# A half-width sort with the rest counted apart, and gathers in threes that wait for TensorE's experts instead of for their own landing

## The reference, cut to what matters

```python
h = (x_flat @ W_gat).reshape(M, 4, 4)
src = concatenate([edge_index[0], loops]); dst = concatenate([edge_index[1], loops])
e = leaky_relu(a_src[src] + a_dst[dst], 0.2)
ee = exp(e - segment_max(e, dst)[dst])
denom = segment_sum(ee, dst)
agg = segment_sum(h[src] * (ee / denom[dst])[:, :, None], dst) + b_gat
scores = layernorm(agg).mean over heads      # then top 2 of 4 experts, softmax
out = sum over experts of gate * (gelu(x @ W1[e] + b1[e]) @ W2[e] + b2[e])
```

## Time and profile before

| | us |
|---|---|
| median of 3 runs | 3851.6 |
| profiled execution | 3831.2 |
| its span, first to last instruction | 3829.6 |
| busy: VectorE | 2878.4 (75%) |
| busy: TensorE, matmuls | 2611.3 (68%) |
| busy: ScalarE | 1816.2 (47%) |
| busy: GpSimd | 1133.4 (30%) |
| mean granted TensorE clock | 0.842 of full speed |

### The profile page before, as it was taken

One profiled execution on the slowest core, in us unless ns is written; L12 is line 12 of the kernel. 1 busy time (PEld: TensorE's weight loads), 2 busy tenths in 40 slices (PEclk: granted clock), 3 DMA queues, 4 the chain that ended last, 5 costly groups with the idle time before them and its releaser, 6 DMA issues.

```text
span 3829.6 us, 50716 instructions
## 1 busy us (share of the span) xinstructions
PE 2611.3 (68%) x16023; PEld 1941.3 (51%) x16024; DVE 2878.4 (75%) x7979; ACT 1816.2 (47%) x3236; POOL 1133.4 (30%) x1200
## 2 busy tenths in 40 slices
PE   2888888888888720015667677676776767676689
PEld 1666666666666510013445455455554545455566
DVE  7999898988898652347777778777777787687774
ACT  1666666666666401112444445344444544444444
POOL 0000000000000014555545555455545555455400
PEclk7999999999999965556878788787878878788889
DMA  2111111111110123222222223223222222322200
GB/s 86 36 48 39 45 39 45 36 36 45 37 47 28 65 23 85 47 60 55 57 73 64 72 61 75 61 59 75 58 72 65 61 71 64 71 61 57 73 12 9
DMA packets 241379, 208.18 MB, mean 54 GB/s; under 512 B 86460, under 2 KB 174168, under 8 KB 240600
## 3 DMA queue, kind: packets, MB, share of 16 engines
q1 hardware_dynamic: 186984, 188.72, 16.9%
q0 software_dynamic: 37152, 14.34, 3.8%
q10 hardware_dynamic: 16976, 1.89, 0.6%
HBM read 158.15 MB, written 46.67 MB: 53 GB/s over the span
## 4 chain that ended last, share of the span: by engine, by line
POOL 23%; DMA 19%; issue 16%; PE 3%; DVE 2%; ACT 0%; POOLq 0%; DVEq 0%
POOL lay_got L1514 23%; DMA lay_got<-node_table,lay_idx 19%; PE lay_b_y L1563 1%; PE lay_b_z L1554 1%; DVE keep_x L1904 0%; DVE lay_xn L1939 0%; DVE lay_stats L1928 0%; POOLq L1512 0%; PE lay_b_b L1593 0%; ACT lay_att L1742 0%; PE lay_b_g L1627 0%; ACT L1686 0%; ACT lay_hid L1686 0%; PE lay_b_g L1643 0%; PE lay_b_g L1635 0%
## 5 line engine op out<-in xcount | busy, mean ns | idle before, releaser
L1514 POOL DMA_INDIRECT lay_got<-node_table,lay_idx x1152 | 1114.3, 967 | 1061.8 <-DMA lay_got<-node_table,lay_idx 827.4
L1563 PEld LDWEIGHTS lay_b_y<-lay_w,lay_hid 128*128 128x128 f32 x4096 | 547.0, 209 | 242.8 <-issue 198.3
L1686 ACT ACTIVATE lay_hid<-lay_b_z,lay_b 128x512 f32<-128x512 f32 x512 | 335.6, 682 | 597.4 <-PE lay_b_z L1554 580.7
L1563 PE MATMUL lay_b_y<-lay_w,lay_hid 128*128 128x128 f32 x4096 | 548.2, 291 | 77.7 <-DVE keep_x L1904 61.6
L1554 PE MATMUL lay_b_z<-lay_xin,lay_w 128*128 128x512 f32 x1024 | 591.6, 707 | 2.0 <-ACT lay_hid L1686 2.0
L191 DVE TENSOR_TENSOR sort_keys<-sort_keys 128x1024 f32<-128x1024 f32 (+1 forms) x272 | 399.0, 1467 | 11.3 <-DVE front_rms L109 0.5
L1540 PE MATMUL lay_b_att<-lay_parts,lay_oh 128*128 128x60 bf16 x1152 | 69.1, 215 | 494.5 <-DVE lay_parts L970 491.5
L192 DVE TENSOR_TENSOR sort_keys<-sort_keys 128x1024 f32<-128x1024 f32 (+1 forms) x272 | 397.4, 1461 | 0.0
L801 POOL MEMSET find_no_src<- 128x9 int32 x1 | 0.1, 108 | 1322.1 <-POOLq L46 1322.1
L1764 ACT ACTIVATE lay_unused<-lay_hub_wide,lay_halves 128x1152 bf16<-128x1152 uint16 x256 | 319.9, 1250 | 140.9 <-DMA lay_hub_wide<-sorted_dst 136.6
L961 DVE TENSOR_REDUCE lay_look<-lay_b_att 128x36 f32<-128x108 f32 x128 | 34.1, 267 | 446.3 <-DMA lay_got<-node_table,lay_idx 445.8
(11 more groups left out here) (344 smaller groups left out, 4832.2 us busy)
## 6 DMA issues: line engine op xcount, KB each, us to landing
lay_wide<-sorted_dst SPq DMA_DIRECT2D x128, 288.0 KB
lay_hub_wide<-sorted_dst SPq DMA_DIRECT2D x128, 288.0 KB
made<-front_y SPq DMA_DIRECT2D x128, 256.0 KB, 2.0
lay_y<-made SPq DMA_DIRECT2D x32, 1024.0 KB, 7.5
lay_got<-node_table,lay_idx POOLq DMA_INDIRECT x1152
front_adj<-in_adj SPq DMA_DIRECT2D x32, 256.0 KB, 3.1
keep_x<-in_x SPq DMA_DIRECT2D x32, 256.0 KB, 3.4
lay_adj<-in_adj SPq DMA_DIRECT2D x32, 256.0 KB
```

The costliest lines, as they stand in the source:

```text
L1514: pool.indirect_dma_start(out=got[:, b % RING, c, :], out_offset=None, in_=table, in_offset=bass.IndirectOffsetOnAxis(ap=idx[:, b % AHEAD, ...
L1563: mm = pe.matmul(b_y[n % 2][:, P * j:P * j + P], hid[n % 2][:, c, P * j:P * j + P], w2[:, e * HK + c, :], start=(c == 0), stop=(c == HK - 1))
L1686: act.activation(hid[n % 2][:, c, :], b_z[c][:, :], ACT.Gelu, bias=b1[:, e * HK + c:e * HK + c + 1]).then_inc(hid_ready, 1)
```

## The change

**The sort at half width.** `Network` now takes 2048 columns and 18 bits. The stages inside a row still sort all 4096 columns, as two halves of 2048. One stage of distance 2048 then leaves the 2048 lowest keys of each row in the left half; the right half is the rest. `set_aside` brings the 128 lowest keys of the rest to its front. Only the left half goes through the 7 levels across rows. Within a part between two turnings only the first and the last stage are taken by halves of 1024, the others whole. TensorE turns 2 quarters for each half instead of 4.

```diff
+            pos = self.run(pos, 0, 2 * cols, [1 << j for j in reversed(range(k))], first=True, directed=True)
+        pos = self.run(pos, 0, 2 * cols, [cols], first=True)
+        for kind, n in (("rest", 2 * cols), ("sign", cols // 2)):
...
+def set_aside(v, me, bufs, scratch, net, pos):
+    here, at = bufs[pos][:, net.cols:], 0
+    n = net.cols // 2
+    while n >= P:
+        low = bufs[1 - pos][:, net.cols:net.cols + P] if n == P else scratch[:, at:at + n]
+        me.mark(v.tensor_tensor(low, here[:, 0:n], here[:, n:2 * n], ALU.min))
+        me.mark(v.tensor_tensor(bufs[1 - pos][:, net.cols + n:net.cols + 2 * n], here[:, 0:n], here[:, n:2 * n], ALU.max))
+        me.wait()
+        here, at, n = low, at + n, n // 2
...
-                    for q in range(4):
+                    for q in range(net.quarters):
```

**The edge tables** store the far terms of each node too, and run a loop over the columns of the rest before the old loop:

```diff
+            act.wait_ge(exps_done, 3)
+            act.dma_start(rest_far[0:nodes, :].rearrange("(t n) f -> n t f", n=P), far[:, :, :]).then_inc(far_out, 16)
             act.wait_ge(table_out, 16)
             act.dma_start(hub_row[:, :], table[nodes - 1:nodes, :].broadcast_to([P, TAB])).then_inc(hub_in, 16)
+            n = rest_count_of(act)
+            with act.Fori(0, n) as g:
+                act.wait_ge(rest_step, 4 * g + 1)
+                act.dma_start(rest_key[:, :], rest_keys[:, bass.ds(g, 1)], allow_slow_non_contiguous=True)\
...
+            with pool.Fori(0, n) as g:
+                pool.wait_ge(rest_step, 4 * g + 2)
+                for out, array, at, got_it in ((rest_row, table, rest_src, rest_got[0]),
+                                               (rest_far_of, rest_far, rest_dst, rest_got[1]),
+                                               (rest_sum_of, rest_sums, rest_dst, rest_got[2])):
+                    pool.indirect_dma_start(
...
+                pool.wait_ge(rest_step, 4 * g + 4)
+                pool.indirect_dma_start(
+                    out=rest_sums, out_offset=bass.IndirectOffsetOnAxis(ap=rest_dst[:, 0:1].bitcast(U32), axis=0),
+                    in_=rest_msg[:, :], in_offset=None).then_inc(rest_out, 16)
+                pool.wait_ge(rest_out, 16 * g + 16)
```

**The layers** add `rest_sums` in the scores (a load of 8 blocks' rows by SyncE and one addition by VectorE), and count the hub edges set aside in rounds -1 and 0: VectorE makes two one-hots of 8 x 128 columns 16 times, TensorE multiplies them in 8 matmuls each into the bank `b_b`, and VectorE adds the result to `more_hub`. The gathers:

```diff
+                n = E1 * ((b - RING - 2) // 4 - QUAD - 2) + 2 * ((b - RING - 2) % 4)
                 for c in range(GC):
+                    if c % 3 == 0 and c > 0:
+                        after(pool, z_done, HK * min(n + 1 + c // 3, groups * E1) if n >= 0 else 0)
                     pool.indirect_dma_start(
                         out=got[:, b % RING, c, :], out_offset=None, in_=table,
                         in_offset=bass.IndirectOffsetOnAxis(ap=idx[:, b % AHEAD, c:c + 1].bitcast(U32), axis=0))\
                         .then_inc(gathered[b % RING], 16)
-
-                    if c % 3 == 2:
-                        pool.wait_ge(gathered[b % RING], (16 * GC) * (b // RING) + 16 * (c + 1))
```

More of the change, by code:

```diff
@@ L140, in __init__ @@
-        for k in levels:
-            t = len(self.holds)
-            self.holds.append(pos)
-            for h in range(2):
-                after = self.run(1 - pos, h * half, half, [1 << j for j in reversed(range(k - row_bits))],
-                                 directed=k < bits, turn=8 * t + 4 * h + 4)
-            after = self.run(after, 0, cols, [half], first=False)
-            pos = self.halves(after, half, [P << j for j in reversed(range(4))])
+            pos = self.run(pos, 0, 2 * cols, [1 << j for j in reversed(range(k))], first=True, directed=True)
@@ new lines, in __init__ @@
+        pos = self.run(pos, 0, 2 * cols, [cols], first=True)
+        self.rest = 1 - pos
+        for kind, n in (("rest", 2 * cols), ("sign", cols // 2)):
+            self.stages.append(Stage(self.total, pos, 0, n, 0, False, False, 0, False, kind))
+            self.total += n
+        pos = self.ends(1 - pos, [1 << j for j in reversed(range(row_bits))], turned=0)
+        for k in range(row_bits + 1, bits + 1):
+            self.holds.append(pos)
+            pos = self.ends(1 - pos, [1 << j for j in reversed(range(k - row_bits))]
+                            + [P << j for j in reversed(range(row_bits - 7))],
+                            turned=2 * len(self.holds) - 2, first=True, directed=k < bits)
@@ L149, in __init__, with run @@
             self.holds.append(pos)
-            pos = self.halves(1 - pos, half, [1 << j for j in reversed(range(7)) if k < bits or 1 << j >= LOOSE],
-                              turn=8 * t + 8)
+            pos = self.ends(1 - pos, [1 << j for j in reversed(range(7)) if k < bits or 1 << j >= LOOSE],
+                            turned=2 * len(self.holds) - 2)
         self.final = pos
         self.turned_from = [s.start for s in self.stages if s.half]
-    def run(self, pos, lo, n, distances, first=True, directed=False, turn=0, half=False):
+    def run(self, pos, lo, n, distances, first=False, directed=False, turn=0, half=False):
@@ L161, in run, with ends @@
         return pos
-    def halves(self, pos, half, distances, turn=0):
-        for h in range(2):
-            after = self.run(pos, h * half, half, distances, first=False, turn=turn and turn + 4 * h + 4, half=True)
-        return after
+    def ends(self, pos, distances, turned, first=False, directed=False):
+        half = self.cols // 2
+        last = len(distances) - 1
+        for i, d in enumerate(distances):
+            if 0 < i < last or not (self.holds or i):
+                pos = self.run(pos, 0, self.cols, [d])
+                continue
+            for h in range(2):
+                after = self.run(pos, h * half, half, [d], first=first and i == 0, directed=directed and i == 0,
+                                 turn=0 if i else self.quarters * (turned + h + 1), half=i == last)
+            pos = after
+        return pos
+def set_aside(v, me, bufs, scratch, net, pos):
[7 more added lines that the diff above has]
+        here, at, n = low, at + n, n // 2
 def exchange(v, me, bufs, stage):
@@ L1241, in rank, with layers @@
     me.link(v.tensor_reduce(out, beat, AX.X, ALU.add))
-def layers(nc, adj, sorted_src, sorted_dst, first, table, made, w, keep, out):
+def layers(nc, adj, sorted_src, sorted_dst, rest_sums, first, table, made, w, keep, out):
     x, acc, far_parts = keep["x"], keep["acc"], keep["far"]
@@ L1575, in expert, with count_rest @@
                 down(g, e)
+            def count_rest(n):
+                pe.wait_ge(rest_ready, n + 1)
+                for c in range(RC):
+                    mm = pe.matmul(b_b[:, 0:tiles], rest_hots[n % 2][:, 0, c, :], rest_hots[n % 2][:, 1, c, :],
+                                   start=(n == 0 and c == 0), stop=(n == P // RC - 1 and c == RC - 1))
+                mm.then_inc(rest_used, 1)
             def turn_gates(n, g):
```

282 lines of the change are left out of this document (225 added, 57 removed).

## The result

The kernel after took 3784.0 us (median of four runs, 3779.7 to 3785.2), the one before 3853.8 (four runs, 3848.0 to 3858.2): ratio 0.982, 95% interval 0.981 to 0.984. The forecast was 3504 us, range 3430 to 3630. So the kernel is 1.8% faster, a small but clear gain, where 9% were forecast.

The account below looks back on a forecast made before the run. It took TensorE's and ScalarE's chain to bound the front and GpSimd's gathers with landing waits the layers. From 3831.2 us profiled, -48 -13 +34 -321 gives 3483; adding 20.4 for the median gives 3504 us, range 3430 to 3630.

Parts of the forecast that it names:

- Front, -48: The 32 sorted groups: TensorE's and ScalarE's chain sets the pace, so mainly fewer turns save time; -48 us, from -10 to -80.
- Finding the blocks, -13: Stretch after the front: halved passes, counts and tables save more than the added work costs; -13 us, from -16 to 0.
- Edge tables, +34, range to +50: Stretch before the layers: an added store of 16-byte pieces and one loop pass, all in series; +34 us, from +17.
- Layers, first 24 blocks, -124: Start of the layers: gathers without landing waits at 11.3 us a block; -4, -90 and -30 us.
- fourth rival: Layers: back-to-back gathers stretch while VectorE runs at doubled rate, to 15.4 us a block; 3610 us, chance 0.05.
- Layers, steady, 67.8 to 60.0 a round, -195: 25 rounds of 4 blocks: GpSimd leaves the chain, its new wait costs nothing, VectorE's round limits; ends -258 and -70 us.
- first rival: Layers' steady rounds: TensorE and the experts' chain hold the round at 65 us; 3629 us in all, chance 0.16.
- fifth rival: Layers: the new wait ties GpSimd to TensorE, so a block's third triple lands too late; 4116 us, chance 0.03.

Follow-up runs that it names:

- first run: The kernel after as first measured and profiled, on a chip not on record: 3784.0 us, ratio 0.982 to the kernel before.
- e5: The kernel after, nothing changed, on another chip than the first experiments: 3525.1 us, ratio 0.920 to the kernel before.
- e9: The kernel after, nothing changed, on a further chip: 3530.1 us.
- e10: The kernel after, nothing changed, on one more chip: 3529.6 us.
- e4: The kernel after with eight of nine gathers left out from block 28 on, for timing alone: 3519.7 us.
- e1: The kernel before with only GpSimd's new waits on TensorE's experts in place of landing waits inside a block: 3511.2 us, ratio 0.914.
- e12: The kernel after without GpSimd's waits inside a block, rest_far stored by partition, dropped edges scattered to their own rows: 3942.5 us, ratio 1.027 to the kernel before.
- e2: The kernel after with the old landing waits by threes in place of the waits for the experts: 3825.9 us, ratio 0.995 to the kernel before.

## Why the prediction was wrong, step by step

- **Front, -48:** right (1324.7 to 1278.4, -46). The last 20 groups lost 40.2 us where 38 were forecast, groups without turns stayed at 36.2 with VectorE idle. Group 0 lost 4.5 where 9 were forecast, though VectorE's work there fell by 9.2 as counted; that the sum is so near is in small part luck. That the sort was beside the chain and only its turns cost time was the reading that mattered: it works 285 us less.
- **Finding the blocks, -13:** right (-13).
- **Edge tables, +34, range to +50:** too small: +67 in the first run, +57 in e5. Two terms were mis-sized. The store of 16-byte pieces was priced at 14 us; it delayed the hub row by 29 us in the first run (VectorE's wait 10.9 to 39.9) and 24 in e5. The nearest row had 96-byte pieces and stood alone; here the second store's pieces queue behind the first's. And the scatter was priced as a gather, 4.1 us; it took 22.8 (20.4 in e5), since all 128 lanes hold dropped edges with one target.
- **Layers, first 24 blocks, -124:** -34 in the first run, with signals held up to 37 us; -102 on time (338.5 us against 440.6 from the end of the edge tables). The first 16 blocks gave 76 of their 90 us in e5: 12.2 us a block, not 11.3, because gathers were longer than the 0.94 us taken (see the fourth rival).
- **Layers, steady, 67.8 to 60.0 a round, -195: the step that failed on the record,** -12. "So it costs nothing, and late next is VectorE's own round" holds where signals are on time: 60.1, 60.2 and 60.3 us in e5, e9 and e10, 59.8 nearly without gathers. In the first run they were not on time, and the round was 67.3. What the step had at nothing is the delay of TensorE's signals by gathers without a landing wait between them: taking those waits away let VectorE and ScalarE wait for TensorE's signals instead. The first rival's round (65) is nearer, but its 3629 is still 155 us short, and its cause is wrong: TensorE and the experts' chain don't hold it there by themselves, as e4 shows.
- **The fourth rival** (gathers stretched by VectorE, to 15.4 us a block): its mechanism is there, at a quarter of its size. In the first 16 blocks of e5, 31 of 143 gathers last over 1 us, together 15.5 us more than at the others' 0.945 each, which is about what the forecast's -90 lacks. e1, which has no one-hots for the counting, takes 188.5 us for these blocks against 195.3. 28 of the 31 overlap one of VectorE's one-hots, and none of the 31 gathers beside which VectorE is idle lasts over 0.96 us. Two long ones and a short one, with VectorE's row (e5):

```profile
1489.53 1.26 POOL L1713 DMA_INDIRECT lay_got<-node_table,lay_idx  x1 [0.30 <-issue]
1491.02 1.22 DVE L2059 TENSOR_TENSOR lay_hid<-lay_iota_b,keep_hub_node 128x1024 bf16<-128x1024 bf16 x1
1491.09 1.97 POOL L1713 DMA_INDIRECT lay_got<-node_table,lay_idx  x1 [0.30 <-issue]
...
1495.86 0.95 POOL L1713 DMA_INDIRECT lay_got<-node_table,lay_idx  x1 [0.30 <-issue]
```

  The prediction read the mean over all gathers (967 ns) and found the rule small; over the whole kernel it is (990 ns in the first run, 1000 in e5), but not where GpSimd sets the pace. In the steady rounds it costs nothing, since GpSimd waits there anyway.
- **The fifth rival** (tied to TensorE, slower): not by the wait. A kernel slower than before did come, in e12, by leaving the wait away on a chip with late signals.
- **Sum with e5's sizes:** -47 -13 +57 -304 = -307 us from a profiled 3831; e5's profiled run took 3525. The forecast's -348 was 13% too much, nearly all in the edge tables and the first blocks. That 3504 lies only 21 us under e5 is in part luck: half of the 41 us was made good by the 20.4 us added for the median, and in e5 the median and the profiled run are the same. But where signals are on time the forecast's steady rounds and its range held.

Could it be foreseen? The kernel before's own trace, from the first setting, has 23% of TensorE's signals late in runs of only three gathers, in semaphore events that I had not read: I read the ends of matmuls. The landing waits hid it, for GpSimd bounds that round at 67.8 us either way (e2, with signals on time, has the same 67.8). How much they would grow without the waits, nothing before the change told. What stays open: what in a chip or a session makes signals late, what holds them, and how short a break suffices.

## What to carry to other kernels

A kernel in which one engine waits at every step can hide something that shows only when the waits go, and only on some chips. Before pricing their removal, compare the times at which semaphores are updated with the ends of the instructions that raise them, and time the change on more than one chip. Long runs of gathers without a break are a risk on some chips and worth nothing once the other engines bound the round. A break of 1.2 us after every third gather won 317 us on such a chip; a shorter one cost nothing on a chip with signals on time and was not tried on the other sort. And a cost that seems small in the mean can stand exactly where its engine sets the pace: read it there, as the gathers beside VectorE's one-hots show. Small pieces of DMA are priced by what stands in the queue behind them, and a scatter by how many of its rows share a target.

## What the runs showed of the hardware that I had not expected

- In three settings of eight TensorE's signals reached the others late while GpSimd issued gathers back to back: in the first run all 25 of the transposes L1817 by 3.2 to 8.7 us (7.8 in the middle), one signal by 37.4 us. Most came when GpSimd paused (342 of 488). The same kernel took 3525 to 3530 us on three chips and 3784 in two settings; without its waits 3521 to 3526 us with signals on time, and 3940 to 3942 with late ones although its edge tables took 45 us less.
- In these settings VectorE's semaphore updates were hit too: 2823 recorded of 4309 in the steady rounds of the first run, 4306 of 4309 in e5.
- With late signals TensorE's granted clock was lower too (0.81 against 0.85): the same matmuls took 4.5 us a round longer, and its idle time grew by 2.7.
- A gather lasted 0.94 to 0.96 us beside an idle VectorE and up to 2.0 us beside its one-hots of 1024 and 1152 columns (e5).
- A scatter of 128 rows of 80 bytes to one row lands in 20.4 to 22.8 us, to 128 rows in 2.2.
- A load of 12 KB behind 16384 pieces of 16 bytes on its queue: 25.9 to 31.1 us to landing, its issue itself 21.5 to 24.8; behind 128 pieces of 2 KB 2.5.
